# Attention with a planned order of steps: the copy of projected k and v is placed straight behind its projection, and four small inversions move to other steps

## What is computed

```python
q, k, v = x @ Wq, x @ Wk, x @ Wv            # per head: 1024 x 128
q, k = q * cos + rotate_half(q) * sin, k * cos + rotate_half(k) * sin
attn = softmax(where(causal, q @ k.T * scale, min))
x = layernorm(x + (attn @ v * head_scale) @ Wo)
# start of the experts' part, which the plan mixes into the second sequence's attention
x_ln = layernorm(x) * gamma + beta           # both norms of a row are folded into one factor
x_n  = x_ln / max(norm(x_ln), eps) * scale
mu_n = mu / max(norm(mu, axis=0), eps)
```

## Time and profile before

| | us |
|---|---|
| median of 3 runs | 1222.25 (1220.8 to 1222.49) |
| the profiled execution's own time | 1219.74 |
| its span | 1217.9 |
| TensorE busy in the span | 1141.2 (94%) |
| VectorE, ScalarE, GpSimd busy | 811.7, 790.7, 710.9 |
| granted TensorE clock, mean | 0.984 |

### The profile page before, as it was taken

The page is one execution under the profiler, slowest core; times in us unless marked ns, Lnnn a source line. Parts: engine busy times, 40 slices in busy tenths (PEclk is TensorE's granted clock), DMA queues, the critical chain, the costliest instruction groups (busy, mean ns, idle before and its releaser), DMA issues. The chain is left out here.

```text
span 1217.9 us, 23566 instructions
## 1 busy us (share of the span) xinstructions
PE 1141.2 (94%) x8096; PEld 1048.8 (86%) x8096; DVE 811.7 (67%) x1899; ACT 790.7 (65%) x1654; POOL 710.9 (58%) x485
## 2 busy tenths in 40 slices
PE   4899999999989999999989999999899989888997
PEld 3798999898989998999989989998778879787986
DVE  5565676566677567666666756776776666776677
ACT  2666676665666667778667766664588777455664
POOL 2767667667675765786757675630178635534541
PEclk9999999999999999999999999999999999989999
DMA  3331211112211112111211111200101010000101
GB/s 99 83 108 45 56 33 44 31 29 54 50 27 32 44 38 51 44 32 27 49 46 38 31 45 36 49 6 19 36 22 31 23 31 19 18 23 14 48 15 36
DMA packets 48789, 47.57 MB, mean 39 GB/s; under 512 B 13080, under 2 KB 43288, under 8 KB 48416
## 3 DMA queue, kind: packets, MB, share of 16 engines
q1 hardware_dynamic: 48384, 45.99, 14.6%
q10 hardware_dynamic: 288, 0.07, 0.0%
HBM read 24.03 MB, written 2.10 MB: 21 GB/s over the span
## 5 line engine op out<-in xcount | busy, mean ns | idle before, releaser
L536 PE MATMUL ring<-kT,qT 128*128 128x384 f32 (+5 forms) x1152 | 245.7, 349 | 9.8 <-ACT exps L701 3.9
L701 ACT ACTIVATE exps<-ring,neg_max 128x128 f32<-128x128 f32 (+7 forms) x256 | 189.2, 742 | 61.4 <-DVE neg_max L845 60.7
L845 DVE CUSTOM_DVE_ANT_0 ring<-ring,hidden 128x128 f32<-128x128 f32 (+7 forms) x256 | 191.4, 767 | 34.0 <-PE ring L536 33.3
L536 PEld LDWEIGHTS ring<-kT,qT 128*128 128x128 f32 x1152 | 186.3, 190 | 22.6 <-issue 5.4
L718 ACT ACTIVATE exp_parts<-turned 128x512 fp32r<-128x512 f32 x192 | 114.4, 596 | 134.9 <-PE turned L551 113.0
L551 PE MATMUL turned<-ident,exps 128*128 128x128 f32 x1152 | 178.7, 273 | 8.6 <-DVE exp_parts L863 4.5
L572 PE MATMUL mix<-exp_parts,v_parts 128*128 128x256 f32 x1152 | 183.8, 295 | 0.4 <-DVE exp_parts L863 0.4
L551 PEld LDWEIGHTS turned<-ident,exps 128*128 128x128 f32 x1152 | 141.6, 141 | 26.7 <-issue 7.4
L863 DVE TENSOR_TENSOR exp_parts<-turned,exp_parts 128x512 fp32r<-128x512 f32 x192 | 131.7, 686 | 33.2 <-ACT exp_parts L718 33.1
L973 POOL TENSOR_TENSOR cos_part<-taken,cos_sb 128x1024 f32<-128x1024 f32 x38 | 91.3, 2402 | 99.6 <-ACT taken L669 99.6
L572 PEld LDWEIGHTS mix<-exp_parts,v_parts 128*128 128x128 f32 x1152 | 148.8, 189 | 0.6 <-DVE exp_parts L863 0.6
(11 more groups left out here) (224 smaller groups left out, 2182.9 us busy)
## 6 DMA issues: line engine op xcount, KB each, us to landing
rotated<-taken SPq DMA_DIRECT2D x76, 256.0 KB, 3.7
raw_q<-in_L_attn_Wq_dram SPq DMA_DIRECT2D x32, 128.0 KB, 3.6
raw_o<-in_L_attn_Wo_dram SPq DMA_DIRECT2D x32, 128.0 KB, 3.4
ffn_mu_next<-in_L_ffn_mu_dram SPq DMA_DIRECT2D x28, 128.0 KB, 2.6
y_sb<-in_L_attn_x_dram SPq DMA_DIRECT2D x2, 1024.0 KB, 7.1
exps_and_mu<-in_L_ffn_mu_dram SPq DMA_DIRECT2D x1, 2048.0 KB, 8.0
ffn_w_sb<-in_L_ffn_W_dram SPq DMA_DIRECT2D x8, 256.0 KB
ffn_w_sb<-in_L_ffn_W_dram SPq DMA_DIRECT2D x14, 128.0 KB, 2.8
```

What stands on the lines that cost most here:

```text
L536: last = nc.tensor.matmul(ring_cols(item, half * BANK, piece), qT[:, H % QUERIES, a, i * P:(i + 1) * P], kT[:, G % 2, m, half * piece:(hal ...
L701: nc.scalar.activation(dst, tile, ACT.Exp, bias=neg_max[:, H % 2, i:i + 1], scale=-1.0, accum_out=row_sum[:, H % 2, i:i + 1]).then_inc(don ...
L845: nc.vector.tensor_tensor_reduce(tile, tile, later, -1.0, 3.0e38, ALU.add, ALU.min, neg_max[:, H % 2, i:i + 1]).then_inc(done[kind], 1)
```

## The change

`take` of k and of v is put into the plan straight after `project`, at n = 9, ahead of the next head's first `diag_hi` and behind nothing but the projection itself. (At n = 9 it so also stands ahead of `mu_sums`, `row_squares`, `turn_unit` and `unit_hi`, which follow in `early`.) `take` of q, and all `swap` and rope products, stay deferred. `mu_inv` moves from n = 3 to n = 6 of head 12; `row_inv_1` and `row_std_2` from n = 2 to n = 6 of head 17; `row_inv_2` from n = 4 to n = 9 of head 17; `row_scale` from n = 4 to n = 9 of head 22. No instruction is added or taken away.

```diff
     def rope(who, n):
         plan.append(("project", who, n))
-        deferred.extend([(kind, who, n) for kind in ("take", "swap", "times_cos", "times_sin", "rope_add")])
+        (plan if who == "k" else deferred).append(("take", who, n))
+        deferred.extend([(kind, who, n) for kind in ("swap", "times_cos", "times_sin", "rope_add")])
...
-        if H == 12 and n == 3:
+        if H == 12 and n == 6:
             plan.append(("mu_inv",))
...
-        if r == 1 and n == 2:
+        if r == 1 and n == 6:
             plan.extend([("row_inv_1",), ("row_std_2",)])
-        if r == 1 and n == 4:
+        if r == 1 and n == 9:
             plan.append(("row_inv_2",))
...
-        if r == 6 and n == 4:
+        if r == 6 and n == 9:
             plan.append(("row_scale",))
...
             if place == 2:
-                plan.append(("project", "v", G + 1))
-                deferred.append(("take", "v", G + 1))
+                plan.extend([("project", "v", G + 1), ("take", "v", G + 1)])
```

## The result

The changed kernel takes 1211.47 us in the median of 6 runs (1208.64 to 1213.25) against 1222.37 for the kernel before (6 runs, 1220.8 to 1226.26). The ratio is 0.9906, with a 95% interval of 0.9889 to 0.9924: 0.9% faster. The forecast was 1211.3. The time is right within a fifth of a microsecond, and yet its terms are not: the copies gave 3.4 us more than forecast, the moved inversions 2.8 less, and the experts' part, put down as unchanged, took 1.7 longer. The rest of this text is about that.

What follows compares the result with a forecast made beforehand. Attention was taken as bound by TensorE, busy 777.4 of 800 us. Copies -5.4, row_scale -5.15, mu_inv -2.2 and first inversion +1.8 make -10.95, so 1222.25 goes to 1211.3 (1210 to 1213, chance 0.48).

Steps and rivals of the forecast that it cites:

- the ring's order: Attention: order of banks makes scores wait for k's and v's copies of groups 2, 3 and 7; six waits go, -5.4 us.
- For the eight other copies: 0: Attention: the other eight moved copies gain nothing, as their scores land on banks freed long before.
- The cover of `diag_lo`: Head 13: diag_lo ends 4.5 us before its reader turns, so its delay by a copy (1.03) costs nothing.
- The slower rival: diag_hi held behind the copy becomes the path at all 14 places, 1.03 us each: 1231.1 us; chance 0.03.
- row_scale: Head 22: leaving its old place gains 5.15 us; at n = 9 a stall up to 4.8 us costs 0.
- mu_inv at n = 6: Head 12: leaving the old place gains 5.15 us; the last instruction stalls behind rope_lo, costing 2.95.
- Rival 1: New places free: mu_inv's last instruction slips ahead of rope_lo, 1208.4 us; were the first inversion free too, 1205.5; together chance 0.2.
- The first inversion at n = 6: Head 17, row_inv_1 and root: the old 1.07 us wait goes, turning and projection waits cost 2.85; loses 1.8.
- rival 2: The clock falls at the new waits in attention: one fall gives 1212.9 us, two 1214.5; chance 0.15.
- The experts' part starts earlier and is unchanged: After attention: the experts' part only starts earlier and adds no term to the forecast.
- The sum: Whole kernel: -5.4 - 5.15 - 2.2 + 1.8 = -10.95 us, median from 1222.25 to 1211.3.
- The Trainium skill's rule on the shared ports: VectorE instructions with two SBUF inputs, or two-port tensor_scalar, fully block while a GpSimd instruction holds the shared ports.

Runs made afterwards that it cites:

- the copies alone: Against the changed kernel, all moved inversions and row_scale are back at their old steps, only k's and v's copies stay moved: 1212.1 us against 1222.98, ratio 0.9913.
- inversions alone: Against the changed kernel, k's and v's copies are deferred again, only the small inversions stay moved: 1216.31 us against 1222.98, ratio 0.9952.

## Why the prediction was right, and where it wasn't

- **The mechanism of the copies** was right: six waits, by the ring's order, and all gone. **Their size was not**: 5.4 forecast, 8.8 in the heads. One part is how I priced a wait: I took the idle time that its row names, 0.85 and 1.0, but to a head each was worth 1.11 and 1.28 (7.0 in sum), as the copies alone show. The other part, 1.8, is a step that I left out, in heads 2 and 14. I wrote that the swap and `times_cos` start up to 1 us sooner and went no further; that they release a queue there wasn't followed. "For the eight other copies: 0" is the sentence that failed.
- **The cover of `diag_lo`** held: no wait for it of more than 0.2 us. The slower rival didn't come.
- **row_scale**: -5.15 forecast, -5.0 measured, with the stall nearly as long as before and hidden.
- **mu_inv at n = 6**: the forecast said which instruction would stall, behind which product, and that TensorE would wait 1.75 and 1.2. Measured 1.65 and 0.88. Without a fall the head's gain is 2.2, as forecast (inversions alone). Rival 1, a slip into a gap, didn't happen in any of the three traces with that place.
- **The first inversion at n = 6**: 0.6 and 2.25 forecast, 0.57 and 1.95 measured; +1.8 forecast, +1.57 without a fall.
- **The clock**: rival 2, one fall or two at the new waits, had a chance of 0.15. In the profiled execution both happened, and in the second profile of the same kernel one of two. They cost 1.4 to 1.6 each, as put. So this rival came true, in the traces of this kernel at least.
- **"The experts' part starts earlier and is unchanged"** failed in both traces of the changed kernel, by 1.7 us, through a fall that no rival named.
- **The sum**: 3.4 more from the copies stand against 3.0 for two falls in attention and 1.7 for the third. The agreement of the median within 0.2 us is luck. The forecast for the profiled execution, 1208.8, was 2.35 below the 1211.15 measured: it was met only in the median, for which the prediction added the 2.5 by which the profiled execution before had been faster than its median, while this one was only 0.3 faster. By parts the forecast was good to a quarter of a microsecond wherever the clock stayed up, and 3.4 us off at the copies.
- **The Trainium skill's rule on the shared ports** (SBUF — State Buffer, Who interferes with whom) spoke against the new places, and the runs agree with it: 2.31 us beside `rope_lo`, 0.23 without it. The about 2.7 us that the Trainium skill gives for a table load (ScalarE: Activation LUTs, Terms) is more than twice what the traces have: every load here took 1.28, and in the rows of head 17 the next instruction starts 0.01 to 0.02 behind it where it has nothing else to wait for.

## What to carry to other kernels

Ask of a moved step what it holds up behind itself at the new place, and, if it is a small VectorE instruction, what GpSimd runs beside it. A chain of small instructions costs nothing only where its whole queue waits for something else anyway: `row_scale` took 3.9 us beside a projection for free, and a root with its table loads vanished there, while the root's chain and `mu_inv` at n = 6 cost 2.9 to 4.6 us against their place at n = 9. And follow an earlier start to the end of its chain, also at the places where nobody waited for the moved step itself.

## What was new about the hardware

A wait that TensorE's row gives as 0.85 us idle was worth 1.11 us, and one of 1.01 was worth 1.27 to 1.28: without it the next matmuls started 0.17 before the modelled end of the former ones and took 0.10 less. And the clock fell in one execution after two waits of 1.65 and 0.88 us and stayed up in another after 1.67 and 0.88: near such a point an edit's price is uncertain by some 1.5 us, whatever is known of its waits. It also fell 44 us behind the end of attention, in five traces of ten, where the waits just ahead were the same to 0.03 us. So the time of a part that an edit doesn't touch has to be read too.
